# Selective-scan kernel, front phase: layer-norm sums split into a high and a low part, two matmuls each, and their chain placed later

## What is computed

```python
xf = group_norm(x).reshape(B, C, -1).transpose(0, 2, 1)      # 4096 positions x 512 channels, twice
mu = jnp.mean(xf, -1, keepdims=True)
var = jnp.mean(jnp.square(xf - mu), -1, keepdims=True)
xn = (xf - mu) * jax.lax.rsqrt(var + EPS) * ln_w + ln_b
xin, z = jnp.split(xn @ in_proj_w.T, 2, axis=-1)             # 1024 channels each
u = silu(causal_conv_4_taps(xin) + conv_b)
x_dbl = u @ x_proj_w.T                                       # 32 of dt, 16 of B, 16 of C
delta = softplus(x_dbl[..., :32] @ dt_proj_w.T + dt_proj_b)
```

## Time and profile before

| | |
|---|---|
| median of 3 runs | 4529.04 us (4528.37 to 4529.25) |
| the profiled execution | 4530.1 us |
| its span, first to last instruction | 4528.2 us |
| mean granted TensorE clock | 0.991 |
| PE busy | 4348.7 us (96%) |
| DVE busy | 3843.5 us (85%) |
| ACT busy | 2959.2 us (65%) |
| POOL busy | 2893.4 us (64%) |

### The profile page before, as it was taken

One profiled execution on the slowest core, in us unless ns is written; L12 is line 12 of the kernel. 1 busy time (PEld: TensorE's weight loads), 2 busy tenths in 40 slices (PEclk: granted clock), 3 DMA queues, 4 the chain that ended last, 5 costly groups with the idle time before them and its releaser, 6 DMA issues. The chain is left out here.

```text
span 4528.2 us, 110691 instructions
## 1 busy us (share of the span) xinstructions
PE 4348.7 (96%) x46908; PEld 2907.6 (64%) x46908; DVE 3843.5 (85%) x3971; ACT 2959.2 (65%) x6420; POOL 2893.4 (64%) x1319
## 2 busy tenths in 40 slices
PE   4999999968999999999999999999997999999999
PEld 3777777745555555555555555555554888887887
DVE  6877777589999999999999999999995888887332
ACT  3667766667877787778778877877774554553111
POOL 1233322279999999999999999999993222221000
PEclk9999999989999999999999999999998999999999
DMA  4654555443233323333332333233321212213443
GB/s 177 221 199 177 193 193 182 170 148 93 81 100 105 102 83 99 99 95 95 104 103 80 100 104 102 83 99 98 98 85 66 84 56 84 84 65 131 186 186 149
DMA packets 195467, 538.60 MB, mean 119 GB/s; under 512 B 15424, under 2 KB 15440, under 8 KB 185504
## 3 DMA queue, kind: packets, MB, share of 16 engines
q1 hardware_dynamic: 190032, 482.40, 33.0%
q0 software_dynamic: 4944, 49.12, 2.7%
HBM read 329.09 MB, written 202.38 MB: 117 GB/s over the span
## 5 line engine op out<-in xcount | busy, mean ns | idle before, releaser
L1039 POOL TENSOR_TENSOR sc_hc<-sc_hc,sc_c_rep 128x1024 f32<-128x1024 f32 x1024 | 2386.8, 2381 | 96.4 <-ACT sc_state L1052 71.7
L1239 DVE TENSOR_TENSOR_SCAN sc_hc<-l_m,sc_state,sc_ring 128x512 f32<-128x512 f32 x2048 | 2417.0, 1282 | 11.2 <-PE sc_ring L1166 5.6
L1084 ACT ACTIVATE l_m<-l1s_v,l_neg_a 128x512 f32<-128x512 f32 x2048 | 1354.7, 709 | 12.0 <-DMA l1s_v<-spill 12.0
L1166 PEld LDWEIGHTS sc_ring<-sc_diag,l1s_iota 64*64 64x64 f32 x32768 | 897.2, 133 | 446.3 <-issue 443.7
L1166 PE MATMUL sc_ring<-sc_diag,l1s_iota 64*64 64x128 f32 x32768 | 1032.5, 274 | 41.7 <-DVE sc_hc L1239 40.1
L1176 PE MATMUL sc_y_ps<-sc_hc,sc_fold 128*64 128x512 f32 x4096 | 935.4, 598 | 1.6 <-POOL sc_hc L1039 1.6
L1176 PEld LDWEIGHTS sc_y_ps<-sc_hc,sc_fold 128*64 128x64 f32 x4096 | 271.3, 136 | 484.8 <-issue 464.2
L1052 ACT ACTIVATE sc_state<-sc_hc 128x2 f32<-128x2 f32 x1024 | 207.6, 203 | 488.0 <-DVE sc_hc L1239 485.7
L1504 POOL TENSOR_TENSOR l_count<-l_count,as_oh 128x1024 f32<-128x1024 f32 x64 | 154.2, 2409 | 526.2 <-DVE as_oh L1707 526.2
L906 PE MATMUL sc_o_ps<-l_et,l_sums 128*128 128x512 f32 x960 | 464.0, 606 | 4.4 <-ACT sc_b_col L1062 4.4
L70 PE MATMUL fr_mm<-fr_xn_hi,l0f_w_in_hi 128*128 128x512 f32 x1024 | 405.8, 396 | 12.1 <-DVE fr_xn_lo L678 9.8
(11 more groups left out here) (204 smaller groups left out, 5763.1 us busy)
## 6 DMA issues: line engine op xcount, KB each, us to landing
sc_duz<-spill SPq DMA_DIRECT2D x128, 768.0 KB, 6.0
l1s_v<-spill SPq DMA_DIRECT2D x256, 256.0 KB, 4.2
spill<-fr_z SPq DMA_DIRECT2D x64, 512.0 KB, 3.4
spill<-fr_u SPq DMA_DIRECT2D x32, 1024.0 KB, 6.0
spill<-l0f_delta SPq DMA_DIRECT2D x32, 1024.0 KB, 5.2
spill<-l0f_du SPq DMA_DIRECT2D x32, 1024.0 KB, 6.4
sc_c_rep<-bc SPq DMA_DIRECT2D x128, 256.0 KB, 4.5
soft<-l_et SPq DMA_DIRECT2D x16, 2048.0 KB, 6.2
```

The source lines that it names most:

```text
L1039: nc.gpsimd.tensor_tensor(hc[:, p], hc[:, p], c_rep[:, 2 * q:2 * q + 2, :], ALU.mult).then_inc(s_hp, 1)
L1084: nc.scalar.activation(da[:, p % 4, r, :], delta[:, i % 2, p % 2, :], ACT.Exp, scale=keep.neg_a[:, c:c + 1]).then_inc(s_da, 1)
L1166: done = nc.tensor.matmul(to[:, :, k::4], dut[rows, i % 2, k, HALF * h:HALF * h + HALF], diag[rows, u, 4 * q + c:4 * q + 4:2, k, :], start ...
L1239: nc.vector.tensor_tensor_scan(hc[:, p, r, :], da[:, p % 4, r, :], ring[:, SLOT[at], r::2], state[:, i, 2 * p + r:2 * p + r + 1], ALU.mult ...
```

## The change

The sum over four blocks goes to a corner of `sq` in place of `half`. ACT then rounds it to fp32r (`sum_hi`), POOL (DVE in the first chunk) subtracts that from the sum (`sum_lo`), and the mean and the variance are each two fp32r matmuls against a rounded copy of the 1/512 matrix (`over`). On PE the mean moves from behind z0 to behind x1, the variance from behind z2 to behind x3. On ACT and DVE the steps behind them move by about one place. Line numbers of the changed kernel are up to 21 higher in `front`.

```diff
@@ pool
             def add_blocks(t, n):
-                nc.gpsimd.tensor_tensor(half[:], t[:, 0:2, :], t[:, 2:4, :], ALU.add).then_inc(s_half, 1)
-                pool.wait_ge(s_half, n + 1)
-                nc.gpsimd.tensor_tensor(half[:, 0, :], half[:, 0, :], half[:, 1, :], ALU.add).then_inc(s_pre, 1)
+                nc.gpsimd.tensor_tensor(sq[:, 0:2, :], t[:, 0:2, :], t[:, 2:4, :], ALU.add).then_inc(s_half, 1)
+                pool.wait_ge(s_half, 2 * n + 1)
+                nc.gpsimd.tensor_tensor(sq[:, 0, :], sq[:, 0, :], sq[:, 1, :], ALU.add).then_inc(s_half, 1)
+                pool.wait_ge(s_hh, n + 1)
+                nc.gpsimd.tensor_tensor(hl[1][:], sq[:, 0, :], hl[0][:].bitcast(F32), ALU.subtract).then_inc(s_pre, 1)
@@ act
+            def sum_high(n):
+                act.wait_ge(s_half, 2 * n + 2)
+                if n % 2:
+                    act.wait_ge(s_mu, n // 2 + 1)
+                elif n:
+                    act.wait_ge(s_var, n // 2)
+                nc.scalar.activation(hl[0][:], sq[:, 0, :], ACT.Copy).then_inc(s_hh, 1)
...
             norm_v(0)
+            nc.scalar.activation(over[:], keep.mean_w[:], ACT.Copy)
+            sum_high(0)
             for k in range(2):
                 high_weights(k)
             square(0)
+            sum_high(1)
...
                 silu_z(g, 0)
+                if more:
+                    sum_high(2 * g + 2)
                 if g:
                     softplus(g - 1, 0)
                 keep_x(g, 1)
+                silu_u(g, 0)
                 if more:
                     square(g + 1)
                 silu_z(g, 1)
-                silu_u(g, 0)
                 keep_x(g, 2)
                 silu_u(g, 1)
                 silu_z(g, 2)
+                if g:
+                    softplus(g - 1, 1)
+                if more:
+                    sum_high(2 * g + 3)
+                keep_x(g, 3)
+                silu_u(g, 2)
                 if more:
                     root(g + 1)
                 if g == PARAMS + 1:
                     group_root()
-                if g:
-                    softplus(g - 1, 1)
-                keep_x(g, 3)
-                silu_u(g, 2)
                 silu_z(g, 3)
                 keep_x(g, 4)
                 silu_u(g, 3)
-                if more:
-                    high(g + 1)
                 silu_z(g, 4)
                 keep_x(g, 5)
                 silu_u(g, 4)
+                if more:
+                    high(g + 1)
@@ pe
-                nc.tensor.matmul(st_ps[:], keep.mean_w[:], half[:, 0, :], start=True, stop=True).then_inc(s_mu, 1)
+                nc.tensor.matmul(st_ps[:], over[:], hl[0][:], start=True, stop=False)
+                nc.tensor.matmul(st_ps[:], over[:], hl[1][:], start=False, stop=True).then_inc(s_mu, 1)
...
                 project(g, "z", 0)
-                if more:
-                    mean(g + 1)
                 if g:
                     project_dt(g - 1, 0)
                 project(g, "x", 1)
+                if more:
+                    mean(g + 1)
                 project(g, "z", 1)
                 project(g, "x", 2)
                 project(g, "z", 2)
-                if more:
-                    var(g + 1)
                 if g:
                     project_dt(g - 1, 1)
                 for m in range(3, 6):
                     project(g, "x", m)
+                    if m == 3 and more:
+                        var(g + 1)
                     if (g, m) == (PARAMS, 4):
                         group_mean(g)
                     project(g, "z", m)
@@ dve
                 conv(g, 2)
+                conv(g, 3)
                 if more:
                     invert(g + 1)
...
-                conv(g, 3)
+                conv(g, 4)
                 if more:
                     normalise(g + 1)
-                conv(g, 4)
-                if more:
-                    low(g + 1)
...
                 conv(g, 5)
+                if more:
+                    low(g + 1)
```

More of the change, by code:

```diff
@@ L245, in front @@
         xb = w.sb("xb", [P, KC, T])
-        half = w.sb("half", [P, 2, T])
+        hl = [w.sb("sum_hi", [P, T], F32R), w.sb("sum_lo", [P, T], F32R)]
+        over = w.sb("over", [P, P], F32R)
         odd = w.sb("odd", [2 * RANK, T])
@@ L266, in front @@
         s_half = w.sem("half_summed")
-        s_pre = w.sem("blocks_summed")
+        s_hh = w.sem("sum_hi_done")
+        s_pre = w.sem("sum_lo_done")
         s_mu = w.sem("mu_done")
@@ L557, in mean @@
                     pe.wait_ge(s_xd, g - 1)
-                nc.tensor.matmul(st_ps[:], keep.mean_w[:], half[:, 0, :], start=True, stop=True).then_inc(s_mu, 1)
+                nc.tensor.matmul(st_ps[:], over[:], hl[0][:], start=True, stop=False)
+                nc.tensor.matmul(st_ps[:], over[:], hl[1][:], start=False, stop=True).then_inc(s_mu, 1)
             def var(g):
                 pe.wait_ge(s_pre, 2 * g + 2)
-                nc.tensor.matmul(st_ps[:], keep.mean_w[:], half[:, 0, :], start=True, stop=True).then_inc(s_var, 1)
+                nc.tensor.matmul(st_ps[:], over[:], hl[0][:], start=True, stop=False)
+                nc.tensor.matmul(st_ps[:], over[:], hl[1][:], start=False, stop=True).then_inc(s_var, 1)
             def group_mean(g):
@@ L747, in add_first @@
             def add_first(t, n):
-                nc.vector.tensor_tensor(half[:], t[:, 0:2, :], t[:, 2:4, :], ALU.add).then_inc(s_half, 1)
-                dve.wait_ge(s_half, n + 1)
-                nc.vector.tensor_tensor(half[:, 0, :], half[:, 0, :], half[:, 1, :], ALU.add).then_inc(s_pre, 1)
+                nc.vector.tensor_tensor(sq[:, 0:2, :], t[:, 0:2, :], t[:, 2:4, :], ALU.add).then_inc(s_half, 1)
+                dve.wait_ge(s_half, 2 * n + 1)
+                nc.vector.tensor_tensor(sq[:, 0, :], sq[:, 0, :], sq[:, 1, :], ALU.add).then_inc(s_half, 1)
+                dve.wait_ge(s_hh, n + 1)
+                nc.vector.tensor_tensor(hl[1][:], sq[:, 0, :], hl[0][:].bitcast(F32), ALU.subtract).then_inc(s_pre, 1)
             def low_weights(k):
@@ L1444, in assign @@
         s_ct = w.sem("counted")
-        s_zc = w.sem("count_zeroed")
-        s_zs = w.sem("sums_zeroed")
         st_e = [w.sem(f"softmax_stored{i}") for i in range(2)]
@@ L1495, in _ @@
         def _(pool):
-            nc.gpsimd.memset(keep.count[:], 0.0).then_inc(s_zc, 1)
-            pool.wait_ge(s_zc, 1)
+            nc.gpsimd.memset(keep.count[:], 0.0).then_inc(s_ct, TT + 1)
             def main(g, u, i, after, first):
@@ L1505, in main @@
                                             ALU.add).then_inc(s_ct, 1)
-            pool.sem_inc(s_ct, TT + 1)
             chunks(pool, main)
@@ L1662, in _ @@
         def _(dve):
-            nc.vector.memset(keep.sums[:], 0.0).then_inc(s_zs, 1)
-            dve.wait_ge(s_zs, 1)
+            nc.vector.memset(keep.sums[:], 0.0).then_inc(s_ad, 2)
+            dve.wait_ge(s_ad, 2)
             dve.sem_inc(s_oh, 2)
-            dve.sem_inc(s_ad, 2)
             dve.sem_inc(s_vl, 1)
```

## The result

| | before | changed |
|---|---|---|
| median of 4 runs (lowest to highest) | 4529.15 us (4528.37 to 4529.49) | 4577.31 us (4576.72 to 4580.76) |
| the profiled execution, span | 4528.2 us | 4575.2 us |
| mean granted clock | 0.991 | 0.986 |

The ratio is 1.0104, 95% interval 1.0092 to 1.0116: the change made the kernel 48 us **slower**. The forecast was 4565 us in a range of 4547 to 4586, slower with 0.91.

What follows compares the result with a forecast made beforehand. PE was taken to bound `front`. Chunks 1 to 14 +24.5 us, start +5, chunk 0 -1.6 and clock +8 gave +36 us on 4530.1, 4566; the runs' median is 1.1 lower, so 4565 us, range 4547 to 4586.

Steps and rivals of the forecast that it cites:

- What bounds: In `front`, chunks 1 to 14, PE is busy 768.51 of 771.00 us, so any wait put on it adds in full.
- the wait that decides: PE at the variance waits for POOL's low part, held by ACT's rounding behind four softplus: 2.65 us a chunk.
- T: The end of z2 on PE, from which the forecast counts the variance's chain.
- The savings: PE, each chunk: cheaper matmuls -0.80 us, z3's wait for a bank gone -0.41, two short waits +0.2.
- The two short waits: x1 waits for z0's bank and x3 for z2's: about 0.1 us each, 0.2 us added.
- Rival 4: Mean and variance: the fp32r pair is no cheaper than the float32 passes, 4577 us; chance 0.05.
- rival 1: PE's clock falls at every variance wait in chunks 1 to 14: 4580 us; chance 0.18.
- The table load: ACT's softplus table load ahead of the rounding costs 1.28 us alone, without the skill's further drain of about 1380 ns.
- The start: Before chunk 0, `sum_high(0)` and a second copy hold back ACT's weight roundings: about +5 us, between 3 and 6.
- The clock: After variance waits PE's clock falls to half for 3.4 us, counted in 5 of 14 chunks: +8 us, bounds 0 and 23.
- The edits costed at nothing: ACT's table load and copies, the later mean and convolutions on DVE, POOL's subtractions: covered by slack, no cost.
- rival 2: The variance's wait is covered, -1.0 us a chunk, +3.4 at the start: faster, 4518 us; chance 0.05.

Runs made afterwards that it cites:

- The filled wait: Changed kernel with ten unread fp32r matmuls put on PE between x3 and the variance in chunks 1 to 14; 4559.6 us.
- the kernel that reached it: Changed kernel with variance behind z3, first chunk's sums in float32, and ACT's norm of v split around the first dt copy; 4518.4 us.
- the split alone: Split arithmetic in the order of the kernel before, ACT's roundings ahead of the silus of z0 and z2; 4562.6 us.

## Why the prediction was right

**What bounds, and the wait that decides.** Right. PE wanted the squares' low part at T + 3.75 and got it at T + 6.4 by the forecast; it went on at T + 6.45. Its pace would have had it at T + 3.73, so it lost 2.72 us (forecast 2.65); the profile's 2.58 counts from the end of the last matmul. The two operations that no row had shown took 0.63 us (rounding, forecast 0.6) and 1.27 us (subtraction, forecast 1.29). Moving the rounding by 1.2 us moved the wait by 1.2, and moving PE past z3 removed it.

**The savings.** Right in sum: where the clock held, a chunk grew by 1.71 us, forecast 1.75. In the run with the variance behind z3 the shortest period is 50.45 us, 0.97 below before, against a forecast of -1.0 without the wait. The terms can be read from the starts on PE. The pair for the mean takes 463.54 - 463.08 = 0.46 us where the float32 one had 0.85, so both together save the 0.80 that I gave. z3 follows the variance 0.23 us behind its second matmul, so its 0.41 us are saved too. The two short waits, for which I added 0.2 us, came to 0.05. The loss at the variance was 2.75 + 0.11 us in the chunk without a fall, 0.1 over the forecast, and makes up for that.

Rival 4, a pair no cheaper than the float32 passes, had given 4577 us, just what was measured, and rival 1 4580. The time alone would not tell them apart. The 0.46 us rule rival 4 out, and the clock records speak for rival 1.

**The table load.** Right. The load took 1.28 us and the softplus followed 1.30 behind its start, as in the kernel before. With the drain of 1.38 us of the Trainium skill ("ScalarE: Activation LUTs", "What ACT_TABLE_LOAD costs") PE would have gone on near T + 7.8, as an estimate. It went on at T + 6.45, so here too the trace stands against the rule's total.

**The start.** +4.5 us, forecast +5; chunk 0 -1.7, forecast -1.6.

**The clock: the mis-sized term.** I counted falls in 5 of 14 chunks, +8 us, and 13 fell, 19 us. That accounts for the time being 12 us over the forecast. The argument that failed was that dense matmuls on both sides of the wait would mostly hold the clock; rival 1, a fall at every wait, is what nearly happened. The filled wait shows that it is the waiting: the same chain with PE kept busy has no fall. The Trainium skill ("TensorE: Matmul & The Clock Gate", "HAM oscillation") has an example of a loop in which every wait sends the clock down, but with waits of about 3 to 5 us. I took it for just this case; these waits of 2.6 us are shorter, and the traces decide: 13 of 14 fell.

**The edits costed at nothing.** True in the changed kernel, but with a condition that I did not name: the wait itself gave DVE and ACT the time. I weighed the late last convolution only against `project_x`, which asks late, and not against the group norm and the dt copies that stand behind it on ACT. Once the wait is gone, this costs 1.0 us a chunk, and so my rival 2, faster at 4518 us, would not have come from removing the wait alone: that gave 4531 us. It needed the start and the end of the chunk mended too, and then came to 4518. That the number is the same is luck: rival 2 kept the late start and knew of no second wait, and in the kernel that reached it the start is mended and some of the second wait is left.

## What to carry to other kernels

Splitting an operation on the busiest engine into cheaper ones puts steps on other engines into the chain that it waits for; ask first in whose in-order queue those steps stand, and what is ahead of them there. A short wait on PE can cost more than its length, so when one can't be avoided, its price is to be read from the clock behind it too, and moving another block ahead of the waiting one can be worth more than the saving inside it: here z3 ahead of the variance took 46 us off, and the cheaper matmuls 0.8 us a chunk. And after a wait is removed, look again at everything that was covered by it.

## What the runs showed of the hardware

Longer waits brought more falls of the clock, with dense matmuls on both sides. Waits of 1.41 us: none in 14 chunks. Of 1.74 us: 8 in 14. Of 2.58 us: 13 in 14. Each count is from one profiled execution, and the waits of 1.74 us stand at another place of the chunk, behind z2. Each slow stretch lasted 3.4 us; in the changed kernel it cost 1.3 to 1.6 us, least where the clock fell while PE still waited. In the changed kernel every fall starts 54.6 us, or twice that, after the one before, while the periods of the chunks spread from 54.5 to 55.1; why the falls keep that distance was not tried. In the run with the split alone, where all 14 waits are of one length, the falls come in chunks 1 to 3, 7 to 9, 13 and 14, and none in between. So the length of a wait doesn't settle it alone; where it lies in time seems to matter too, which no run tried apart.

What was not tried: which of the reordered steps on ACT and DVE makes the last convolution late, what the copies add to it with PE's own work kept the same, and waits between 1.74 and 2.58 us.
